# State-space steps of a four-stage model kernel: where the second half of a weight tile stands in TensorE's order

## The reference

```python
proj = input_states @ in_proj_w.T
gate, xBC, dt = proj[..., :INTER], proj[..., INTER:INTER + CONV], proj[..., INTER + CONV:]
xBC = silu(conv4(xBC) + conv_b)
cum = cumsum(softplus(dt + dt_bias) * A)            # within a chunk
scores = (C_i . B_j) * exp(cum_i - cum_j) * dt_j    # j <= i, one matrix per head
y = scores @ x + (C * exp(cum)) @ state + D * x     # state carried from chunk to chunk
g = rms_norm_by_group(y * silu(gate)) * norm_w
return g @ out_w.T
```

## Time and profile before

| | us |
|---|---|
| median of 3 runs | 2231.82 (2231.77 to 2232.87) |
| profiled execution, its own time | 2228.98 |
| its span, first to last instruction | 2227.0 |
| PE busy | 2108.4 (95%) |
| DVE busy | 1462.8 (66%) |
| ACT busy | 1353.2 (61%) |
| POOL busy | 861.2 (39%) |
| mean granted clock of PE | 0.980 of full speed |

### The profile page before, as it was taken

The page is one execution under the profiler, slowest core; times in us unless marked ns, Lnnn a source line. Parts: engine busy times, 40 slices in busy tenths (PEclk is TensorE's granted clock), DMA queues, the critical chain, the costliest instruction groups (busy, mean ns, idle before and its releaser), DMA issues. The chain is left out here.

```text
span 2227.0 us, 37068 instructions
## 1 busy us (share of the span) xinstructions
PE 2108.4 (95%) x12040; PEld 1562.7 (70%) x12040; DVE 1462.8 (66%) x1813; ACT 1353.2 (61%) x2384; POOL 861.2 (39%) x758
## 2 busy tenths in 40 slices
PE   6879999898999999999999999999999987999998
PEld 4634444476777777777777777777777756888886
DVE  4446666284568677778778587786787764555555
ACT  2145555433588878888787787877888762233332
POOL 1011111121157666657666575665667570000000
PEclk9989999999999999999999999999999998999999
DMA  3422322223445445445454454455454557444462
GB/s 132 161 75 71 82 76 61 74 95 95 119 131 161 158 148 175 145 140 184 134 165 154 145 166 154 140 168 153 150 177 148 159 181 256 141 139 139 141 217 76
DMA packets 184055, 310.81 MB, mean 140 GB/s; under 512 B 20512, under 2 KB 96800, under 8 KB 183744
## 3 DMA queue, kind: packets, MB, share of 16 engines
q1 hardware_dynamic: 183872, 308.53, 44.7%
HBM read 252.52 MB, written 55.68 MB: 138 GB/s over the span
## 5 line engine op out<-in xcount | busy, mean ns | idle before, releaser
L145 PE MATMUL ssm_pp<-xhi,ssm_lo 128*128 128x512 f32 x1192 | 479.4, 402 | 4.7 <-DVE ssm_bc L1541 3.5
L147 PE MATMUL ssm_pp<-xhi,ssm_hi 128*128 128x512 f32 x1192 | 466.2, 391 | 0.0
L146 PE MATMUL ssm_pp<-xlo,ssm_hi 128*128 128x512 f32 x1192 | 465.6, 391 | 0.0
L1443 ACT ACTIVATE ssm_sct<-ssm_cumb,ssm_gpar 128x128 f32<-128x128 f32 x1024 | 312.9, 390 | 53.5 <-DMA ssm_cumb<-dt_sums 28.5
L1541 DVE SCALAR_TENSOR_TENSOR ssm_xc<-ssm_pp,vectors,ssm_xc 128x1022 f32<-128x1022 f32 (+2 forms) x192 | 245.1, 1277 | 47.3 <-ACT ssm_xc L1402 32.3
L137 POOL TENSOR_TENSOR ssm_lo<-ssm_raw,ssm_hi 128x512 fp32r<-128x512 f32 x149 | 238.0, 1602 | 93.1 <-ACT ssm_hi L126 93.1
L145 PEld LDWEIGHTS ssm_pp<-xhi,ssm_lo 128*128 128x128 f32 x1192 | 224.0, 188 | 69.0 <-issue 20.9
L147 PEld LDWEIGHTS ssm_pp<-xhi,ssm_hi 128*128 128x128 f32 x1192 | 224.2, 188 | 48.1
L146 PEld LDWEIGHTS ssm_pp<-xlo,ssm_hi 128*128 128x128 f32 x1192 | 224.3, 188 | 42.8
L1576 DVE TENSOR_TENSOR ssm_sct<-ssm_sct,ssm_cbm 128x1024 f32<-128x1024 f32 x128 | 224.5, 1754 | 40.5 <-ACT ssm_sct L1450 27.8
L1708 POOL TENSOR_TENSOR ssm_go<-ssm_t,ssm_gt 128x512 f32<-128x512 f32 x128 | 165.1, 1290 | 201.3 <-DVE ssm_t L1612 201.3
(11 more groups left out here) (210 smaller groups left out, 4011.8 us busy)
## 6 DMA issues: line engine op xcount, KB each, us to landing
ssm_cumb<-dt_sums SPq DMA_DIRECT2D x96, 1024.0 KB, 6.1
ssm_raw<-w SPq DMA_DIRECT2D x149, 256.0 KB, 5.6
gated<-ssm_go SPq DMA_DIRECT2D x128, 256.0 KB, 4.6
out_graw<-gated SPq DMA_DIRECT2D x64, 512.0 KB, 4.2
out_raw<-w SPq DMA_DIRECT2D x65, 256.0 KB, 2.7
ssm_cumb<-dt_sums SPq DMA_DIRECT2D x32, 512.0 KB, 4.0
ffn_raw<-w SPq DMA_DIRECT2D x37, 256.0 KB, 2.8
stk_qs<-qk_parts SPq DMA_DIRECT2D x96, 64.0 KB, 2.2
```

The costliest lines, as they stand in the source:

```text
L145: pe.matmul(out, wlo, xhi, start=start, stop=False)
L146: pe.matmul(out, whi, xlo, start=False, stop=False)
L147: return pe.matmul(out, whi, xhi, start=False, stop=stop)
L1443: i = act.activation(sct[:, s % 2, h, :], cumb[:, s % 2, 0, h, :], ACT.Relu, scale=-1.0, bias=gpar[:, unit, 0, s % NTOK, h:h + 1])
```

## The change

In a step that has one entry, and outside the last pass's linear-layer tiles, the entry is split by batch: its first 12 matmuls stay ahead of the turn, its last 12 (with `tile_done`) go behind the head products of the same step. These are steps 0, 1, 3, 4 and 6 to 14; steps 2, 5 and 15 keep their order. Entry 29 (turn B) stands in step 15 and is not split. No other engine's order is changed.

```diff
             def body(g, last):
                 for s in range(NS):
+                    halves = [e for e in at(s, last) if len(at(s, last)) == 1 and not (last and e >= NE)]
                     for e in at(s, last)[:1]:
-                        entry(g, e, range(1) if last and e >= NE else range(B))
+                        entry(g, e, range(1) if halves or last and e >= NE else range(B))
                     for e in at(s - 1, last):
                         if last and e >= NE:
                             entry(g, e, range(1, B))
                     if s < NS - 1:
                         turn(g, s + 1)
                     scan(g, s)
+                    for e in halves:
+                        entry(g, e, range(1, B))
                     for e in at(s, last)[1:]:
                         entry(g, e)
```

## The result

| | before | after |
|---|---|---|
| median (us) | 2230.18 (12 runs, 2224.93 to 2236.74) | 2238.86 (12 runs, 2237.04 to 2241.72) |
| ratio, 95% interval | 1 | 1.0038 (1.0028 to 1.0048) |
| span of the profiled execution (us) | 2227.0 | 2235.7 |

The change makes the kernel slower by 8.7 us, 0.38%. The forecast had been 3.0 us faster, with a range from 2222 to 2238 us; the result lies 0.9 us above its upper end.

What follows compares the result with a forecast made beforehand. TensorE was taken as the bound, busy 146.05 of 149.00 us a pass, so only its waits could be won. Terms of -5.0 us (`scores` of 13, entry 25) and +2.0 us (restart) gave -3.0 us: 2228.8 us, range 2222 to 2238.

Steps and rivals of the forecast that it cites:

- The wait at step 15 therefore stays: Head products of step 15: their seven waits for `scores` remain, about 2.1 us each, near 15 us in all.
- `silu` of entry 25 later: ACT, ahead of `scores` of 13: this gate's `silu` starts 0.07 us later a pass, in seven passes.
- tile ends later elsewhere (slot of entry 25): Weight tiles: each ends 3.41 us later, but no term was given for entry 25's wait for its slot.
- What shortens that chain: `scores` of step 13: `weigh` on POOL is over by 1047.74, so `scores` takes 1.22 us, not 2.00; -0.78 us a pass.
- What is new on the path: Step 0 after the group loop's restart: head products wait for `scores`, 0.4 us in each of five passes, +2.0 us.
- the last pass: Last pass: its big wait is held by a gate tile of step 5 whose place doesn't move; 0.
- The first term: Chain to step 15: `silu` of entry 25 starts 0.19 us after its tile's end, +0.07 us a pass.
- just covered: Head products of step 14: would start at 1061.66, after `scores` of 14 ends at 1061.02, so no wait.
- The third term: Loop restart, step 0: DVE's five pauses return at full length and head products wait 0.4 us each, +2.0 us.
- The gap wasn't filled: Denies the rival for step 15: `scores` comes 2.80 us earlier and the gap fills, 2214.3 us; chance 0.10.
- POOL's neighbour stays: Rival at `scores` of 13: it keeps 2 us beside a POOL operation, +2.5 us, 2234.3 us; chance 0.22.
- The slower rival: ACT at tile 25: ACT is late, 1.28 us of table load exposed a pass, +6.0 us, 2237.8 us; chance 0.14.

Runs made afterwards that it cites:

- the best kernel: The changed kernel with gates last among ACT's `silu` rows of steps 9 and 12, and the entries of steps 0 and 1 left whole: 2209.67 us, 0.9917.

## Why the prediction was wrong

Each of its steps, for the seven passes, against what the rows show:

| step of the prediction | forecast | measured |
|---|---|---|
| "The wait at step 15 therefore stays" | stays, near 15 us, 2.1 each | 16.9 us in 7, 2.4 each |
| `silu` of entry 25 later | +0.5 | +1.5 |
| tile ends later elsewhere (slot of entry 25) | 0 | +2.0 |
| "What shortens that chain", `scores` of 13 | -5.5 | +2.0 |
| "What is new on the path", loop restart | +2.0 | +2.6 |
| the last pass | 0 | +0.3 |
| clock in step 15 | not spoken of | +1.1 |

The right column adds up to 9.5 us; the span grew by 8.7, and the difference lies ahead of the block and behind it, where nothing was changed (the first opening turn is at 618.85 us before and 617.60 after). The last row is smaller than what kernels with the same wait of 2.4 us differ by (sum of B 67.9 to 79.1), and some 0.7 of the restart's 2.6 isn't clear of its scatter.

**The step that failed is "What shortens that chain".** It gave -5.5 us; measured are +2.0. It took `weigh` of 13 to be over by 1047.74, because it "follows its turn". Its input was ready in time, but the sum of squares stood ahead of it in POOL's queue. The row that would have told so was in the trace of the kernel before, in POOL's timeline of step 12, just ahead of the earlier trace rows:

```profile
1047.29 0.73 POOL L1714 TENSOR_TENSOR ssm_sq<-ssm_sq 128x256 f32<-128x256 f32 x1 [3.13 <-ACT ssm_sq L1455]
```

The sum of squares had 3.13 us of idleness before it and was released by ACT's square; its second row (1048.09, 0.46 us) and then `weigh` (1048.51) followed without a gap. So `weigh` was not bound by its turn before either. Of the 11.7 us between forecast and result this step makes 7.5. The run with `weigh` first shows the size that it was given to be right (1.28 us, against a forecast of 1.22), and the sum of A falls by 7.2 us with it. That this kernel takes 2227.73 us, against a forecast of 2228.8, is luck: it still has the slot wait that wasn't foreseen, its sum of A is 1.0 us longer than before instead of 3.0 shorter, and at the same clock it is no faster than the kernel before.

A second term was put at nothing without a reason: that tiles end later elsewhere too. It measured 2.0 us (the slot of entry 25), and the run with a whole tile at step 8 took just these away.

**The first term** had the right mechanism and sign: `silu` of 25 starts 0.20 us behind entry 26, as said. It was undersized by 0.14 us a pass. In the kernel before, entry 26 came behind the head products, and its first row took 0.34 us to the next instead of 0.23; that start is now spent inside tile 25, which the count of 2.80 us for a half didn't have. What was missed is that the same holds for every gate, not for entry 25 alone. Gate 22 holds ACT at 1015.37 in the same way, and from there it goes through the exponential, `scores` of 10 (3.96 us of waiting) and the convolution to the slot: 0.34 us in six passes. The heads of step 14, said to be "just covered", wait 0.52 us since `scores` of 13 wasn't shortened; hidden, because they are ahead of the big wait.

One reading on the way was half right. `scores` of 13 began when its exponential ended, at 1049.58, but DVE had no gap ahead of it either. This row stood there until 1048.32 + 1.32 = 1049.64:

```profile
1048.32 1.32 DVE L1568 TENSOR_TENSOR ssm_cecl<-ssm_cumb,ssm_cc 128x1024 f32<-128x1024 f32 x1
```

So before the change both held it at once. In the change DVE stands idle for 3.04 us ahead of it, and the exponential alone holds it, as the sum assumed.

**The third term** had the right mechanism: the five pauses of DVE came back (12.5 us against 12.7), and five waits of 2.0 us came with them, as forecast. The size was in part luck. In three kernels with the same step 0 (gate last in 12, in 9 and 12, and `weigh` first) there are 3 or 4 such waits with 0.9 to 1.3 us. The other 0.6 us come at the restart itself, ahead of the heads. What the pause is made of no run here shows.

**The rivals.** The gap wasn't filled (the run with step 14 alone shows why). "POOL's neighbour stays" is what happened, at 7 x 0.27 us worse than its price. The slower rival's sign came true, not its mechanism: the table load at 1039.09 is over at 1040.37 and still hidden.

On SBUF: the Trainium skill ("SBUF — State Buffer", "Who interferes with whom") says that a vector operation with two inputs in SBUF and a GpSimd operation that reads SBUF exclude each other. The runs agree: with the low part begun 0.11 us ahead (1051.16 to 1052.45), `scores` of 13 ends at 1053.54, 1.09 us behind its end, nearly one `scores` alone (1.22 us).

**Open.** Why the clock falls in one pass and not in the next behind the same wait isn't settled; nor was anything tried on it alone. The 2.6 us between time and trace for the best kernel at the same clock (1.5 for the change) have no place either.

## What to carry to other kernels

Splitting a tile brings the scan forward by half a tile (2.8 us here) and puts the tile's end back by the work that now stands inside it (3.4 us and more here). So look for who waits for the whole tile, and in every in-order queue for what stands behind that wait; then put ahead of it the work that waits for nothing. An instruction is early only if all that stands ahead of it in its queue is early too, so before a term is built on "its input comes sooner", read what its engine was idle for just before.

## What the runs showed of the hardware

- A wait of TensorE of 1.9 to 2.4 us in step 15 was followed by a granted clock of 0.50 in some passes: 37 of 63 in nine profiled kernels (all of these waits but one are 2.3 to 2.4 us; after the one of 1.91 us the clock fell too). In the four kernels whose longest wait there was 1.2 to 1.7 us it was none of 28. With the gate last, where the wait went from 2.4 to 1.3 us, the rest of the seven passes became 8.1 us shorter as well.
- `scores` on DVE (128 x 1024, two inputs) takes 1.22 us alone and 1.28 to 2.32 us where a POOL operation has begun just before it or runs beside it. At the end of a chain that is up to 1.1 us from the order of another engine's queue.
